# Inverse deviations of all norms: Ln and Exp on ScalarE in place of a power on GpSimd, with a refitted order

## Chip, cores, metric

The kernel runs on one core of a Trainium2 chip. The metric is device time in microseconds (us) of one execution. The core's engines are PE (TensorE), DVE (VectorE), ACT (ScalarE), POOL (GpSimd) and SP (SyncE, which here only issues DMAs). They run side by side, each in its own fixed order, and wait for each other through semaphores.

## What is computed

Four layers with pre-normalisation over x of 8 batches x 1024 rows x 128 columns, all in float32:

```python
def _layernorm(x, axis=-1, eps=1e-05):
    m = jnp.mean(x, axis=axis, keepdims=True)
    v = jnp.var(x, axis=axis, keepdims=True)
    return (x - m) / jnp.sqrt(v + eps)

x = x + L0_attn(_layernorm(x))   # A: linear attention with decay, 16 heads, a scan over the rows
x = x + L0_ffn(_layernorm(x))    # B: mixture of 8 experts, the best 2 of each row, hidden 352
x = x + L1_attn(_layernorm(x))   # C: conv of 3, silu, selective scan with 16 states, gate
x = x + L1_ffn(_layernorm(x))    # D: mixture of 8 experts (best 2) and 2 shared ones, hidden 128
```

So there are 32 norms, four for each batch; the change touches `1 / sqrt(v + eps)` of each.

## The kernel before

**Stages.** The letters A, B, C, D stand for the four layers. A and C take one batch after the other. B and D run as jobs of one or two batches: the rows of a job are sorted by expert into blocks of 256 slots. For a job, the rows are normalised, the gates computed, the rows scattered to DRAM by indirect DMAs of POOL (`m_scatter`, L866), each block's rows and its expert's weights loaded by SP, multiplied on PE (L908 to L910 up, L1062 down), passed through silu on ACT (L1308, L1315), gated on DVE (L1687, L1698), read out by ACT (L1324), stored, and gathered back into x by indirect DMAs of POOL that add (`m_gather`, L885). The D layer of the last batch is computed densely (all experts for all rows, letter E in the norm's names), so that no scatter or gather stands at the end.

**A norm.** `row_stats` on DVE takes means and variances of the 8 row groups of a batch (L1403, L1407) and adds eps (`ve`, 128 x 8, L1409). `inverse_deviation` on POOL (L845) raises this to the power -0.5 (`rstd`). `shifts` on DVE (L1413) makes -mean x rstd. `normalise` on ACT (L1170) writes x x rstd + shift. Four steps of the order belong to it: `s_stats`, `s_rstd`, `s_shift`, `s_norm` (with m_ for the jobs and d_ for the dense batch).

**The order.** `ORDER` is a string of 4944 letters. Each letter names a chain of steps (A a batch's attention, P a job's preparation, C the selective scan's stage, G the gathers and so on), and each occurrence takes the chain's next step. `program` goes through the resulting plan once for every engine, and each engine takes the steps that it has a function for. So the string fixes the order on every engine, POOL's and SP's queues too. A step that waits holds everything behind it on its engine.

**ScalarE's tables.** An activation function needs its table in the engine; the compiler puts a table load ahead of an activation whose table isn't there (`ACT_TABLE_LOAD`). The softplus of stage C (`c_soft`, L1268 and L1270) is an Exp and then a Ln; the decays (L1279) and the gate scores (L1292) are Exp.

**Waits around the change.** `rstd[s].sem` counts one for each inverse deviation of a layer; `shifts` and `normalise` wait for it. On POOL the power waits for `veps`.

Of the kernel before, what the change touches and what calls it, by code (L numbers as in the profile page):

```python
# [41 lines left out]
class BankUses:  # L42
# [37 lines left out]
    "RALsSMUqKoPNVskLAZkVULUPqoSRMTPsVMUAwoTsLwXXkAVkPoUXKPqUXsLSqAosUKwkAeLqkwoAVXVMSSTkoUqAswXeLUoXwqsPPsAoUqNA"  # L80
    "VkoswAPsNLwoqZwRAVUUqLZsVqwPSowTUeAXPsMqqosULewKwqKANVosUPAAoZPLRPRPqUKMAswqwVVTwwUUAwLPeAAPNLZAPUTANeRLSVMP"
    "KSVUAPLAZUPVPGMUeSTSNPKPAZPPVPGULSPRPAPUNLePGeVARTKAAMZAAUNLSAAPUAPZAVAPGRALeRUATAMLVUNVXTAXAUoVUeKUANLSMZVo"
    "sLskoGAUKqSeUsoALkUqwRANsqRKLZGVGoVTMwsUkoMTqAkKRLUUAVwULkGVZoXsXqoAsTewVUAUNkLsLMKqoUAVqCTCUkXoMwsLUAkeswCw"
    "CwLqoAVUoCCqRSAXSqsqCCZVSwoCCsACUosLUCwCsCCXAXLXKCXCCoCqCNCCVCCZCACAwwCsCqwSoqMXbTcqNXUAsXURZAbLdSVdCwqUewVw"
    "xAwhcwKXXxTeAdNXAAAhbAAbAPLAXApZAMxAUAPcSpALAAxAeAUAbVhXAdVAPpNAUcLXZddAoPhxoysZAKbSNhRyxTMABGcekVRboqKSpcUR"
    "scTNpMdbPUehePLVAqyLyUUkRPsKxLwwopkVMPysPhTZbcRoUUALdPxpPVAKNVTUSZqcPbhNUSLModdyVxqLsKUPAPeUpPVycRThLMbLUoxZ"
    "VswUAkeRUhNLZwdVTqKqUMoRUwbNdsVxLTkAepUVoMLZesqwUkAUVGykocGbsVAwLqsoKNRdqKkhwwMUSATpysUxoweSTUVARbpcKqULZoGe"
    "yLNqhVdRwULsAKsUyoZxsxAwVVbMNULSoeLATqMcUUhbqGZLMTwdpRqNGKoswyVVcUqUswUAeqNVpSTcVUZyhKxwdwALLMUUcpNVyALSZwSG"
    "RALSAPeAUhKAARRPpAAAPKVPeZLyKxUTVUMPUAVPLAPAThPUeUTLNpVMyMCRPPGCPULPVPZACSAUCPUCLCPNLVUCCPVUACCTCPCCAKACMPCC"
    "eULZCXCCXCXXAPCPCXLCAVCCCAAXRXCTACXPCACACKNMoCoAZssobSUAVeCNUCVqUbqPVsULoALXUxLRwPZeNdXcqxPPSkRXoXbUZhAPSMsT"  # L90
    "kSKxdNVedVZboRcSkApLuuhUkllvSeKxTMdNsvhpdAqZwpcTbcyUqyxUwSsnXbLoUKdcAMVkLhSXVLXnhUdykxapeobXLVKUcwXXypcVyshA"
    "NkdsbxZoqXUbPwqRAphcdowNSULUZwsAVRxkTRyLUxwKTeMoULbAebqdsVpUUVqBMwPsoLVPchRTZKNxeSVUNLphPUMRVqLqKwAUcyxZodpP"
    "bTMUyhUNcLsVPAyobSSdsPKpPeRLdAVcUwLUqxLwbeoPUMhTZVRysVAUpcKwhLqVUeSNZTUyxuVRKGhwvpLSuTxMNqswlZlSNyddoeZyGUGc"
    "GMvpqbAhGdLScnsaRnbUwVURKpUxeLVyqTLchMUpxwUKVNyUVULNZRehATKUVLLMypAZAVGUCeCCLUCwAVGRUGCLSCATMNKTVACRSZUUACLN"
    "AVPePUGAKCRMCVSTZLUCCNMUCLUZCeSAPVVLRPUVTULUTCKVMKMUCCVPLAPGCCLPUCUCTSUCMPPKPPCeGPPCPULVCLNPGPCUCPCCCCeAPCCK"
    "ZNRVZPUcTbNLRULeVUUMbXLAXKNVUCVAxZhdcdxZdXSAebAAeXRbXAPpLAAhxUALPTAcpMXAAKVAdoUTPbXVAcMUhNosXSVbyRdXULxLShpy"
    "AUVSsxUopdyLZNAPkXVsZceecxuloSSNUPbvhVZbhqKuNkAnxLSZsyluvdqnoppcyxXudlbRblhvwebcPhPyTxdXaMvwAUXPnhdUSpXLXPcq"
    "oxPnsUXPKTVXphLwsyPcKbKdekXPURaMpLkAcVxPoXGBkRUGqLwbysAcVPqUqphRNGTwKRSZeMoxddpUKAVhyLTcxMeNUbZTRkwMoLkUSVLT"
    "AesNpbVsyyKqcwGRKhZdMqRoNMZTRqGAVSkwNspxeUyoeTAGchqbZMexKGTVULyNdwcMdphxywVoGhpLwepSGZNULKsUsTRAMKySLeyoeCAV"
    "CCSKqsTqSCNRZRMUKowAZCeURVCNLwTGqeKCMVGZwLsUMNoLqTsCZAqKwRwCoVCUseTCGKwSCCqMCwSLPCCCDVSPPZeNTVMCCeCGUCKPCCPU"  # L100
    "GCCGPCCLVGCKCPPGCLNPPeVKCPPKNGSPPBZRPTeeCRCCPMNcRcZTNZPUbRPdMxSGbdZSRLNVPSUbMLhKMTSUXdbexTSVGhdUNRLZxXLXTVNp"
    "VdUKcpRcZhXKTMbPyXLMpTSUSZZLMxVNeZXNhpbdyNVPxcUcLxPPSePhXbeuXpXbVchyPpyXbyXbddXSZXxXPhXpxPlZdycbdXNXcxybycxc"
    "hpxPdXvPubcPhySpulSKnuhpRvvhPxpyylncdxTbUdldhvbMRnLUcyRpanRThxdbpxMXVRUTchGMLcyGGULapUVhKdxphUyeNyZeGSTyMpVL"
    "CRVCGCULUCCCULNTKZVUMKKCSGUVeTNSULCCVCCCURCMRLCLeCCZGUCVPVLUCCCKCeNCCZCRVCCCGUGSTZNCeRLCSUVMUGUCNCLUCKTCGPMe"
# [1668 lines left out]
```

## Time and profile before

| | us |
|---|---|
| median of 3 runs | 1686.34 (1683.7 to 1690.24) |
| the profiled execution, its own time | 1692.46 |
| its span | 1690.1 |

The page's second part shows the span in 40 slices of 42 us; each digit is the busy share in tenths, PEclk the clock granted to PE in tenths of full speed:

```profile
PE   6778999998999869989896578789577865857788
DVE  6897887989997879869994887689689488757946
ACT  2313455467657746676546565685645763576551
POOL 1104040872742864638688768610578567763686
PEclk9997999999999989998998689899878988988999
```

A busy share is a mean over a slice: it says which engine a stretch is near to be filled by, not which wait ends last in it. ACT and POOL wait for others much of the time.

### The profile page before, as it was taken

Reading aid. Unit: us, or ns where it says so; the run is one execution under the profiler, and the core shown is the slowest. Engines: PE = TensorE matmul, PEld = TensorE weight load, DVE = VectorE, ACT = ScalarE, POOL = GpSimd, SP = SyncE. Lnnn points to the kernel's source line nnn. Section 1 sums busy time; section 2 is a strip of 40 time slices with the busy share of each in tenths; the row PEclk is TensorE's granted clock in tenths of the full one; section 3 lists DMA queues with packets and bytes.
Section 4 is the critical chain, followed back from the end, with each engine's and each line's share of the span. In section 5 each row is a group of like instructions: output and inputs, shape, how many; then the busy total and the mean of one; then the engine's idle time right before and its main releaser. Section 6 shows DMA issues by size and latency. Waiting matters only on the chain.

```text
span 1690.1 us, 29123 instructions
## 1 busy us (share of the span) xinstructions
PE 1368.6 (81%) x9192; PEld 921.8 (55%) x9192; DVE 1369.1 (81%) x2543; ACT 944.7 (56%) x1667; POOL 924.9 (55%) x544
## 2 busy tenths in 40 slices
PE   6778999998999869989896578789577865857788
...
DVE  6897887989997879869994887689689488757946
ACT  2313455467657746676546565685645763576551
POOL 1104040872742864638688768610578567763686
PEclk9997999999999989998998689899878988988999
...
GB/s 276 259 11 98 112 182 162 208 173 281 281 248 138 266 196 282 247 210 257 234 219 174 243 241 225 303 299 272 168 266 230 165 207 270 224 220 214 301 126 69
...
## 3 DMA queue, kind: packets, MB, share of 16 engines
...
## 4 chain that ended last, share of the span: by engine, by line
issue 14%; PE 10%; DVE 8%; POOL 8%; DMA 6%; ACT 5%; SPq 1%; POOLq 0%; DVEq 0%; ACTq 0%
POOL x L885 6%; DMA x<-outs,slot_idx 3%; DVE arena_c L1521 2%; DMA arena_c<-bc_rows 2%; POOL rows L866 2%; PE bank L1097 1%; PE bank L1117 1%; DVE arena_c L1516 1%; DMA xg<-rows 1%; DVE arena_c L1507 1%; PE bank L1062 1%; PE bank L990 1%; PE bank L1106 1%; PE bank L908 0%; ACT yrow L1324 0%
## 5 line engine op out<-in xcount | busy, mean ns | idle before, releaser
L885 POOL DMA_INDIRECT x<-outs,slot_idx x240 | 487.8, 2033 | 180.8 <-issue 89.3
L866 POOL DMA_INDIRECT rows<-xrow,slot_idx x240 | 350.9, 1462 | 249.6 <-ACT xrow L1226 94.8
L990 PE MATMUL bank<-arena_c,ident 128*128 128x512 f32 x512 | 270.2, 658 | 73.2 <-DVE arena_c L1507 73.2
L1521 DVE TENSOR_TENSOR_SCAN arena_c<-arena_c 128x1024 f32<-128x1024 f32 x128 | 295.3, 2309 | 1.5 <-ACT arena_c L1279 0.7
L908 PE MATMUL bank<-xT_ring,mix 128*128 128x128 f16 (+1 forms) x1296 | 243.9, 226 | 52.9 <-DVE mix L1698 16.5
L909 PE MATMUL bank<-xT_ring,mix 128*128 128x128 f16 (+1 forms) x1296 | 243.2, 225 | 0.0
L910 PE MATMUL bank<-xT_ring,mix 128*128 128x128 f16 (+1 forms) x1296 | 243.1, 225 | 0.0
L1062 PE MATMUL bank<-mix 128*128 128x128 f32 (+1 forms) x1296 | 183.3, 286 | 34.6 <-ACT yrow L1324 22.5
L1062 PEld LDWEIGHTS bank<-mix 128*128 128x128 f32 (+1 forms) x1296 | 166.7, 198 | 69.5 <-issue 64.5
L908 PEld LDWEIGHTS bank<-xT_ring,mix 128*128 128x128 f16 (+1 forms) x1296 | 139.9, 108 | 97.9 <-issue 69.4
L990 PEld LDWEIGHTS bank<-arena_c,ident 128*128 128x128 f32 x512 | 97.7, 208 | 169.3 <-DVE arena_c L1507 87.9
L941 PE MATMUL bank<-arena_a,Wv 128*128 128x512 f32 x256 | 149.1, 666 | 29.5 <-DVE arena_a L1459 28.5
L1303 ACT COPY xT_ring<-bank 128x512 f16<-128x512 f16 x156 | 90.7, 582 | 135.9 <-PE bank L1037 135.5
L1324 ACT ACTIVATE yrow<-bank,xg 128x128 f32<-128x128 f32 x312 | 96.9, 363 | 120.8 <-PE bank L1062 114.8
L1516 DVE TENSOR_TENSOR arena_c<-arena_c 128x1024 f32<-128x1024 f32 x128 | 154.6, 1211 | 7.9 <-DMA arena_c<-bc_rows 4.8
L1507 DVE TENSOR_TENSOR arena_c<-arena_c 128x1024 f32<-128x1024 f32 x128 | 157.4, 1233 | 4.1 <-DMA arena_c<-bc_rows 3.1
L1279 ACT ACTIVATE arena_c<-arena_c,A_w 128x1024 f32<-128x1024 f32 x128 | 143.9, 1145 | 27.0 <-DVE arena_c L1521 24.7
L950 PEld LDWEIGHTS bank<-Wo,arena_a 128*128 128x128 f32 x1024 | 132.5, 199 | 46.0 <-DVE arena_a L1466 23.2
L950 PE MATMUL bank<-Wo,arena_a 128*128 128x128 f32 x1024 | 141.9, 287 | 17.7 <-DVE arena_a L1466 17.0
L909 PEld LDWEIGHTS bank<-xT_ring,mix 128*128 128x128 f16 (+1 forms) x1296 | 139.9, 108 | 21.2 <-issue 19.9
L910 PEld LDWEIGHTS bank<-xT_ring,mix 128*128 128x128 f16 (+1 forms) x1296 | 140.1, 108 | 0.0
L1698 DVE SCALAR_TENSOR_TENSOR mix<-bank,winv,mix 96x256 f32<-96x256 f32 (+1 forms) x156 | 73.8, 474 | 66.4 <-ACT mix L1315 58.0
...
## 6 DMA issues: line engine op xcount, KB each, us to landing
arena_c<-bc_rows SPq DMA_DIRECT2D x256, 512.0 KB, 5.6
...
rows<-mix SPq DMA_DIRECT2D x3, 2580.0 KB, 13.2
```

Of the source, the lines that this page charges most:

```text
L866: pool.indirect_dma_start(out=xs_d[q % ROW_SETS], out_offset=bass.IndirectOffsetOnAxis(ap=slot_idx[:, q % RJ, c, j:j + 1], axis=0), in_=xr ...
L885: pool.indirect_dma_start(out=x[:, b, j, :], out_offset=None, in_=y_d[q], in_offset=bass.IndirectOffsetOnAxis(ap=slot_idx[:, q % RJ, c, i ...
L908: pe.matmul(o, hi, xh, start=True, stop=False)
L909: pe.matmul(o, hi, xl, start=False, stop=False)
L910: return pe.matmul(o, lo, xh, start=False, stop=True)
L941: filled(f"A{b}.v{k}", pe.matmul(fill(f"A{b}.v{k}"), Wv[:, f, :], half(normA, h), start=True, stop=True))
L950: last = pe.matmul(bank[A_BANKS[1]][:, rows], qs[:, k % RQ, rows], Wo[:, f, :], start=(f == 0 and j == 0), stop=(f == EF - 1 and j == TH - 1))
L990: last = pe.matmul(bank[C_BANKS[h]][:], ident[:], half(hb[:, n % RR, :], h), start=(n == 0), stop=(n == NS - 1))
L1062: last = pe.matmul(o[:, j * P:(j + 1) * P], h_ring[n % RH][0:rows, at:at + P], w2(q, k, j)[0:rows, c, :], start=(c == 0), stop=(c == NC[s] ...
L1507: dve.tensor_tensor(hb[:, n % RR, :], hb[:, n % RR, :], Cb[:, g % RB, :], ALU.mult).then_inc(c_prod.sem, 1)
L1516: dve.tensor_tensor(hb[:, n % RR, :], Bb[:, g % RB, :], w, ALU.mult).then_inc(c_dBx.sem, 1)
L1521: dve.tensor_tensor_scan(hb[:, n % RR, :], dA[:, n % RDA, :], hb[:, n % RR, :], 0.0, ALU.mult, ALU.add).then_inc(c_scan.sem, 1)
```

## The change

The power on POOL goes, with its constant -0.5. ScalarE takes its place: Ln of the variance plus eps, a wait for that Ln, and Exp of -0.5 times it, in the same place. Each inverse deviation now adds two to the semaphore, and who waited for one waits for two. Nothing else of the arithmetic changes. All three steps (`s_rstd`, `m_rstd`, `d_rstd`) move from POOL's program to ACT's.

```diff
-        neg_half = sb("neg_half", [P, TT])
...
-        rstd = {s: signal(f"{s}_rstd_done", 1) for s in "ABCDE"}
+        rstd = {s: signal(f"{s}_rstd_done", 2) for s in "ABCDE"}
...
         def _(pool):
...
-            pool.memset(neg_half[:], -0.5).then_inc(s_cons0, 1)
...
-            def inverse_deviation(s, b):
-                wt.wait_ge(veps[s].sem, veps[s].at(nth_of(s, b), 1))
-                pool.tensor_tensor(rstd_b[s, b % 2][:], ve_b[s, b % 2][:], neg_half[:], ALU.pow).then_inc(rstd[s].sem, 1)
...
             def normalise(s, b, dst, done, tiles):
-                wt.wait_ge(rstd[s].sem, rstd[s].at(nth_of(s, b), 1))
+                wt.wait_ge(rstd[s].sem, rstd[s].at(nth_of(s, b), 2))
...
+            def inverse_deviation(s, b):
+                logs = rstd_b[s, b % 2][:]
+                wt.wait_ge(veps[s].sem, veps[s].at(nth_of(s, b), 1))
+                act.activation(logs, ve_b[s, b % 2][:], ACT.Ln).then_inc(rstd[s].sem, 1)
+                wt.wait_ge(rstd[s].sem, rstd[s].at(nth_of(s, b), 1))
+                act.activation(logs, logs, ACT.Exp, scale=-0.5).then_inc(rstd[s].sem, 1)
...
             def shifts(s, b):
-                wt.wait_ge(rstd[s].sem, rstd[s].at(nth_of(s, b), 1))
+                wt.wait_ge(rstd[s].sem, rstd[s].at(nth_of(s, b), 2))
```

The order string is replaced as a whole. It has the same letters, each as many times; 615 of its 4944 places hold the same letter, the rest are mostly shifted by a few places. Its first line was and is:

```diff
-    "AAAAAAAAAAPAAAAWAAAAAAAWAAAAWAAokAksoWAosqkWAoskksqAoqwAskAwoWwAqqwAwsoqAsowqkkswAwoqsoqsowAsAAwAoqwwqossoAq"
+    "AAAAAAAWAAAAAAWAAAAAAAWAWAAAAAAoAsAoAAsoWqqosWswoAqsAowkqwskAqoqwkskoAqswwkkoAAqskwoqsAokwAAwwAAswowqsoAqqso"
```

## Rows read from the trace of the kernel before

**Rows 1.** the page, part 1, and part 4, the chain by engine.

```profile
PE 1368.6 (81%) x9192; PEld 921.8 (55%) x9192; DVE 1369.1 (81%) x2543; ACT 944.7 (56%) x1667; POOL 924.9 (55%) x544
...
issue 14%; PE 10%; DVE 8%; POOL 8%; DMA 6%; ACT 5%; SPq 1%; POOLq 0%; DVEq 0%; ACTq 0%
```

**Rows 2.** stages of 100 us: busy us of each engine (instructions), granted clock, DMA.

```profile
400.00:500.00 100.00, 92.91 (x801) 70.66 (x801) 99.93 (x124) 58.86 (x99) 47.12 (x15) 1.00 0.86 263
...
900.00:1000.00 100.00, 65.70 (x318) 42.22 (x318) 73.34 (x164) 64.46 (x112) 79.43 (x53) 0.74 0.78 226
...
1200.00:1300.00 100.00, 62.45 (x270) 33.51 (x268) 82.65 (x76) 58.74 (x76) 81.86 (x48) 0.78 0.78 236
```

**Rows 3.** what DVE waited for: us, times, longest.

```profile
DVE mix L1698 <- ACT mix L1315: 58.0, 33, 4.2
...
DVE arena_c L1498 <- ACT arena_c L1270: 16.2, 5, 7.0
...
DVE shift_C L1413 <- POOL rstd_C L845: 11.8, 7, 7.5
...
DVE shift_D L1413 <- POOL rstd_D L845: 6.9, 2, 5.2
```

**Rows 4.** chain of waits, its longest piece: start us, us, what.

```profile
1104.20 79.12 issue
```

**Rows 5.** time line, batch 7 norm C: start, us, instruction [idle].

```profile
1467.61 0.17 DVE L1409 TENSOR_SCALAR ve_C<-mv_C 128x8 f32<-128x8 f32 x1
...
1467.87 1.67 POOL L845 TENSOR_TENSOR rstd_C<-ve_C,neg_half 128x8 f32<-128x8 f32 x1 [7.61 <-DVE ve_C L1409]
...
1469.58 0.17 DVE L1413 SCALAR_TENSOR_TENSOR shift_C<-mv_C,rstd_C 128x8 f32<-128x8 f32 x1 [0.37 <-POOL rstd_C L845]
```

**Rows 6.** POOL by line: busy us, mean ns, idle before.

```profile
L845 POOL TENSOR_TENSOR rstd_B<-ve_B,neg_half 128x8 f32<-128x8 f32 x8 | 17.3, 2166 | 20.4 <-DVE ve_B L1409 20.4
...
L845 POOL TENSOR_TENSOR rstd_C<-ve_C,neg_half 128x8 f32<-128x8 f32 x8 | 14.3, 1789 | 120.4 <-DVE ve_C L1409 120.4
```

**Rows 7.** time line at two shifts that waited for POOL's queue.

```profile
885.62 0.29 DVE L1409 TENSOR_SCALAR ve_C<-mv_C 128x8 f32<-128x8 f32 x1
...
897.91 0.17 DVE L1413 SCALAR_TENSOR_TENSOR shift_C<-mv_C,rstd_C 128x8 f32<-128x8 f32 x1 [7.53 <-POOL rstd_C L845]
...
1223.01 0.17 DVE L1413 SCALAR_TENSOR_TENSOR shift_D<-mv_D,rstd_D 128x8 f32<-128x8 f32 x1 [5.15 <-POOL rstd_D L845]
```

**Rows 8.** time line of ScalarE behind the softplus of batch 5.

```profile
1208.28 1.06 ACT L1270 ACTIVATE arena_c<-arena_c 128x1024 f32<-128x1024 f32 x1
1209.35 1.28 ACT L1279 ACT_TABLE_LOAD   x1
1210.65 1.15 ACT L1279 ACTIVATE arena_c<-arena_c,A_w 128x1024 f32<-128x1024 f32 x1
```

**Rows 9.** ScalarE by line, two of the table-load groups.

```profile
L1279 ACT ACT_TABLE_LOAD x64 | 82.1, 1283 | 1.2
...
L1315 ACT ACT_TABLE_LOAD x42 | 53.9, 1283 | 13.4 <-PE bank L910 12.6
```

**Rows 10.** time line of ScalarE at the start.

```profile
9.53 0.20 ACT L1154 ACTIVATE tanh_base<-cols 128x1 f32<-128x1 f32 x1 [7.45 <-DMA Wo<-in_Wo]
9.63 0.19 ACT L1155 ACTIVATE half_b<-cols 128x1 f32<-128x1 f32 x1
9.86 1.26 ACT L1170 ACTIVATE arena_a<-x,shift_A,rstd_A 128x128 f32<-128x128 f32 x3
```

**Rows 11.** time line of POOL, powers ahead of a gather.

```profile
1318.66 1.67 POOL L845 TENSOR_TENSOR rstd_C<-ve_C,neg_half 128x8 f32<-128x8 f32 x1 [8.13 <-DVE ve_C L1409]
...
1324.72 1.60 POOL L885 DMA_INDIRECT x<-outs,slot_idx  x1 [0.17 <-issue]
```

**Rows 12.** DVE by line, the row statistics.

```profile
L1403 DVE BATCH_NORM_STATS2 row_sums<-x 128x6 f32<-128x128 f32 x256 | 52.3, 277 | 5.0 <-DMA x<-in_x 4.9
```

**Rows 13.** what PE waited for.

```profile
PE bank L1037 <- DMA xg<-rows: 26.1, 13, 11.0
```

More of the change, by code:

```diff
@@ L80 @@
[L80 to L104, printed above, removed]
@@ L120 @@
-    "GQIFJZIFOGFOGQJFQOIGOFGIJOGFFQQIFOGJOGFIOIGIFQOOFOIJGIJFJOFIGIQJOIQIQOJQJQJQQJQJQGQQ"
+    "AAAAAAAWAAAAAAWAAAAAAAWAWAAAAAAoAsAoAAsoWqqosWswoAqsAowkqwskAqoqwkskoAqswwkkoAAqskwoqsAokwAAwwAAswowqsoAqqso"
+    "AWqoAswwwsoqqwwsPAqWAAAwPAWAWAPAPAAAAAAAAAAAAAAAWAkosAAAkoPkqPsoPwqAsoqwAsPoAqskoqkPowssoAkqkswoAPPwkqPPAAwq"
+    "woAwssAoqsowqqosswqCwoAwqAswPoqAswAoAwqsqAPwPwWPAAAAwAAAAPPAAAAAPAAWXXAAXPWWAAAAXkAoCAAskosXKXoKPqAqXoXsAAPo"
+    "seXqkwPwqAkwAweAoAsPoRXsosqoksAwkPPqkwwoqPAsPCoAqwqswoPRsqowqRsAwAwToAUsqoTsPqKkwqUAMLMVLUTVAUwsNMwoqUUPwsLA"
@@ new lines @@
+    "TRqLweVRVPUUNMZLKAAATLVUARUMATUwSULeVAVZAPNMUCLPPKARVeNZLTPAUUKALAARVPMAeVPPZAAUARXXVAAULAAAVAKUALKNUAUSXZos"
+    "TLPMUkAqoVRKNXLZkXAsULSPVTXUPqoMUAkwVTMsALoSPSwsXVkXRUoKqsPqeUALoXUwAKwskSqoAXkUTVVLeAoswoPqUwsksMAPUqNoqAVo"
+    "XkLwRsPLANswoqZULZVwUAqswqVoPSwsTqUPqAoesqUwwKLARNoKRMVUPAsPAoPwXZLPqUseAqVLwTKMeVwwAUNwAPPLZUeAASRAAMTLUPVK"
+    "VNPSULAZPeVPSUPPMPGZSUVKTNAGPPLUGPPSLGPRRAUPeVGePNKAASGTAUARMZAAULPNAZPAAAALVUPAAMLeRVKVAoTUNXAUUVTVUeAeoZsL"
+    "NALsUMUoqXsoAkkGKUqsVwGLARKoXXLZNVRSTsoqwMUTAURkUAUVKwMqLoLkksVZAKSqTLkLwoUsVeXsUCNAKkMXVRUqwqCToUAULoAsMXKw"
@@ new lines @@
+    "CkLwsqCqwUACVCLowCSosCqeACVqZoCCUACssosUXwCoSCCXAXCCCNSCCqZCCLXVXCCCCACAsoSRwCwwqbcqXwTSXNMAZVbUUqeLdXsAwXCK"
+    "XwqAxhUcwwxXpAThddVAAbANeALeAcPASAZAAMAUbpAxAAALAhcAXAdVxVbApAPeZUGdNAdoPhAxyUANLoRhyysxTcZqVbMApPUpoRbKTRcL"
+    "eRbMesNPychKUPdAqVPsLpoSVPwxMUwkTbUsyULPkhUZkeALPPoNAdUTxNVcRUKdVhZykMLSpLUdqoVxPAbsUqpPLVRKPSPohbyTMwLUxVZU"
+    "eAkUcwRNhsKLdZbdVqoMqdRTUkcBwGUsNLVeASxkKTpVwUceosqUAULRVZoSysKsbAGwVLoNTMqkwhAwUqypxsUowVGUAqbUZpRSdVeRoseL"
+    "qcLNywhKMGUTsAoKSxUVZyAwLVxbGMoNsceULTZAhMLqUUqLdSwZTpKRMNobcwVsVUqGqywsAUqdTeVNUpLVwUKLcwyhxUAUSLSpNZcMVSRA"
@@ new lines @@
+    "wLAPyRShAPAAUKAepZPRxAyPSLAVUhTKMUPALVAeUKVAPLVTUUpPTeNMPMyPPCCVRPLPUCCPZAACUCVAULPPNLUCPUACVCCTPCCACCPKAMLC"
+    "eCZUCGXCCCPXCPXCCAACCAVCCLATAPCRXCCAXCoXCANMKAoXZbbNCsAUsoUVCVPRUqULAVsLNLXUeoxZPwcqdXSRPkXPkZxAdehSUosbKPNV"
+    "BTxqMSekVXXoXZAubRucpLhvXSUdlTlXxMdNsdSwUvXhXApKkcXqpyyeqTxUXbwLUZcAsonebdcVUKhVkMLLShbdxcnapVLPwyoUpVbKcsyh"
+    "kUNxbosyRALUqddqSUpZwSAeGRowZwRVsxNAxTkLeKhyGUwToVqMUkALbsbdpVqPUcwsMLoUVTRhVKPwZLNUexpNPhMULVqxdSqhUZcAcGoK"
+    "eyTPULpRysbVUMPNbKASoswLRdcPpdPyAUVUebLwLqwGxoMTPUhcSyRcVsVAUTpZNKGhqULVUxLVyGheZMuRSvSpwuTNxqwKslNoZGvyyblG"
@@ new lines @@
+    "UddpeGcqZAShGRScMsdTnnaUbwVURpxULMecVqhLpyKLUxwUAKRVNyUKVULZehTVNLeLpAwMZAUCVyRUCCULCSACVUTAMKLNCATCUUACACCV"
+    "ZRLPPSMNULeZeVTUACKCRSRUNVKCMLVUGZCPUTSLUVUTVPVKCLMMUCLCPULAPCPCCUPTGUCVKVMCPAPCPPPPULeCNPLCCPeUCCCPACCPKNRZ"
+    "TUVCbNPUCeZLSMUXLRUbXKAXVAVCcLxeVNhcXZRdxdXdAPbAUSZAALXAAbLpUXhAePPxAAcpTKMAcAVXdyPUbTUMAobyVhUosSVdLcLNxXkR"
+    "hASdUpyVUsxeoXNXbLZpuVseAPNxoSZlUbqvhScZuVNhxpsLyovAZSnuKlddlyXRwucpnbkqxclhevbyxPSPhTdaMAPbUXUnXvchdSpLqKox"
+    "XKnUPPLTcBVpskKyXbPXhsadUeMPXRpLPVkwoAxRRkPUwccRyqbLAPsZUqpVqNhToxwMKdeKbdepUAVyTLhMNxoUkcZRpTMbwVLyUTXAwekN"
@@ new lines @@
+    "VGASqcswsKLoMhRdZyVTZKeSqMqZNRSRxsUNypMoTLqcAGhbwweTxUKywNcKyepdGVMhSTxeVohedpLpsKwRZNsUALUoLVyyKSZkeCACTMCG"
+    "SKRNKsCeUVqoRwNZqMCMZLRqTAUCLGVCwsUNSZGoqseVMGKTCKqLGRwosAKCwVTSweqMUGCCCwCwGCKBSCCDSPGPLGUNGVTZCCNGCUeCMCCC"
+    "PPCLCCPPPGeCCVCPLGCPKCPNPePGCSVPKPRGNTZCRPcNZCPePxZMGTMcdGSUZVPRbPbNhdSLRUKZTXTbMLMXxUURSNVhexddLeRLTpKSbTXV"
+    "pVSZdcUMUPhRNcyMTpKbSLxSMVNZehNXZNXLPSypVbxcXUdcexZPPPLehbpbdXVcbXhpXbxuPXKXPydXyXcZddyxySXySlNyPbZhXcdcpXSb"
+    "bXxXhPPPxcpulcxyvRPbhulpnuhpyvhvnxdydbplxTcUhddcnyRMRRvpLahRUnUxphMTcLVXbTULxyKdcaRyUpUVhxpNhGpZyTyGVGCCMGUe"
@@ new lines @@
+    "GVeLPCSLCUUCMLNCTUKVZMKKUCTNVCeURRVLCSCGCUCCCMGGLVULCZCCSCUCCNVLeCCKCZTUeGRSCeCZGRVNCLCSMCCUVUUCCNUTCLCKVebM"
+    "bCPGUGUVVZPLLccKLSxVUbUNxdGRTLhMKVUebPKVUUTyZLxpNLchpRUPdBxbVdPZhTMdULyLUPcVMRNxUGUbeUKZpGLbPVdyhPcxpecLNTUb"
+    "MeRPKVxSULyhZcbVpVdcdhpUTdKNhLyPTUGVMUSbUxShcMRpyLZpcdVNbyxeVLUZeRSPLhUcbUTGdKxyPVbcuLpVeNMhpdKxddyhlZPyTNux"
+    "bvPphbnUyvxZMplcRUdcPUVhxLnKxUydpPePdTLcVShRLUbVUVLcMyKaUNLpPhUUyuyLlSSVpTVZxMhSvupleUZyRNCvReCLCUCNSKeSKUCC"
+    "ZTnnVULCCeVaMUNTPCKGKCCLCUCMCPZVCCCUPCLCXCCPXCCVUXCCNCSCVXCCCCCLLCXSCbxVZUXcbcbhebdcPxpdhexhpKdyxpbNdcbxXcPb"
@@ new lines @@
+    "XXyXhdpXhxPcXZbPdhXdccPdPpPXyySpPSxbhXuXKpXvKyxebehydlbPucXlcpbPevxuhdyyxchuvnRRclpxdRPdyRPpxyTURdTblnvMMTLh"
+    "MhbULTpaKXVpndcecUynxyVBKNhbaLTpUMKdxdhVeZMybNpRcLPPKcZUVRVGxLMShpSZyZTxNNRMSULVGhZNTULRMZeeVTKpyNRUMTVLNZKS"
+    "yRGSeCCUKRLCNCMTCSVCZKULTMRSNTZCVCPUKMSNCCRCUTCKCPCePLMZRTPLCVMCPCPUGNPeZGSTPGeMKeVGCCPCVNGGUCPGKRKGPGVGLPGP"
+    "ZSCSGLCCeCPCUePNCCNCSLRRPVCSZTTCUMZPKMCCNbPuNBSRZPTKLXVcCblvcXxudhUdlpRbMLcvxhUbeLXTeybVpXXndxdGunXMbbhZKpud"
+    "clNZSNxecVTveKbUayvXhMXbXxylcxShKyhdxNdpVcnLSUcpexXbZyneKhSXpayxhSyephcbdVeZxcXSppdNLZKXbXxcyyXhbRTpRdhcxXpd"
@@ new lines @@
+    "XRTdUbxTUXhpcMdMVLbhRcRyLpNKxdZyVMUhdeRXTNKbpcyeMTZUSVNLxyVLhpcMRGUZeGNSxhdLKZyTeVURKRMySZpLRKNyCCGTMVCGNeKC"
+    "TSRUKMCZMTLUCGTKNLGMCPUCTPSCCUVKKVRCVPNZSCCLReLMGZeCCCGCNRZeCCTVCCMSCCGCeCGTeSNGCCUZLCRVCMGCCULVCSTGMTKUCbCU"
+    "bVZGLNNMPULKPRPLVVxxZcRePuSldZbPNvPhpGNxPdduSPKGSNbdZhPcZhxTMcbTRhPUSRPcTlPyRKppMPvPbKnLMxPdcdUpSeXyeKnPGyca"
+    "beVBUeXhVTXLXZbKyNxcXpuxTMVuLSlddUbMKhevehGSveXlNcLxNpXUZynVpbLnVXNSXyxaZbhpSyXSdydcZdcNybxKxTXZhSbcRecpRdhd"
+    "MpdxbeRMKhhGpcRcGReUxLbpTMyyxThMdbUcGVphTyTKKpyLUcNUNGNeLMUZRVZLSyZVTxydUKxMLRhTNySVKpRehGVpKRCVCCCMNUZCNELS"
@@ L121 @@
+    "KZTeMGZERGeSVMLUSEMTTNULUSeEZGVENRKEVGSLEGuZNeVTveuLlENRZUlMGEvVSSnnTuZNLuGUEalZvvnVMnlFFJESLaIOJIFNEOFOFIOZ"
+    "GFOFGOSFGOFFFOSOFIOGFOOGFOFOFGOGGGGGJGGIQJQQIJOJQIQJQJJJIQJQQIJQIJQGQIJGQJQJQQQIIIII"
 )
@@ L820, in ready @@
                 pool.iota(blk_i, pattern=[[1, NBT * MOST_BLOCKS]], base=0, channel_multiplier=0).then_inc(s_cons0, 1)
-                wt.wait_ge(s_cons0, 9 + len(run))
+                wt.wait_ge(s_cons0, 8 + len(run))
                 for m in run.values():
@@ L889, in m_gather @@
                         compute_op=ALU.add).then_inc(gathered[i] if c else gathered_first[j], 16)
-            program({"top": top, "d_rstd": d_rstd, "c_bias": c_bias, "ready": ready, "s_rstd": inverse_deviation, "m_rstd": m_rstd, "m_scatter": m_scatter, "m_gather": m_gather})
+            program({"top": top, "c_bias": c_bias, "ready": ready, "m_scatter": m_scatter, "m_gather": m_gather})
         @block.tensor
@@ L1171, in normalise, with d_rstd, m_rstd @@
                                    scale=rstd_b[s, b % 2][:, j:j + 1]).then_inc(done, 1)
+            def inverse_deviation(s, b):
[4 more added lines that the diff above has]
+                act.activation(logs, logs, ACT.Exp, scale=-0.5).then_inc(rstd[s].sem, 1)
+            def d_rstd(b):
+                inverse_deviation("E", b)
+            def m_rstd(q, i):
+                inverse_deviation(JOBS[q][0], JOBS[q][1][i])
             def s_norm(s, b):
```

29 lines of the change are left out of this document (3 added, 26 removed).

## The prediction

> **What bounds the kernel now.** The executed profile is 1692.5 us, its span 1690.1; the median of three runs is 1686.3, so what I add to the profile I add to the median as well. I read the engines' busy times first [rows 1]: PE and DVE stand at 81% each, ACT at 56%, POOL at 55%. No engine is full over the whole, so the stages come next [rows 2]: from 400 us DVE is busy 99.9 of 100 us and the sum there is DVE's; from 900 and 1200 us neither PE nor DVE is over 83%, and PE's granted clock is 0.74 and 0.78, means between its two levels of 1.2 and 2.4 GHz. There the time is made of waits between engines, and a longer wait costs. Then the waits of DVE and PE [rows 3, 13]. On ACT, DVE waits 58.0 us for the last silu of a block and 16.2 us for the logarithm of the softplus; with the smaller rows of both engines' lists I add up 122 us for DVE and 62 us for PE, 184 us in all. For the norms, DVE waits at the shift 11.8 us (C), 6.9 us (D), and 3.4, 1.9 and 1.8 us (B, E, A): 25.8 us.
>
> The chain of waits passes over POOL for 8% of the span and has 14% "issue" [rows 1]. I don't take this as POOL's price: its longest "issue", 79 us [rows 4], ends at the norm of C at 1183 us, where POOL stood in its queue for a variance that DVE had not reached. That is a wait of POOL, not for POOL.
>
> **What a norm costs now.** In the plain case [rows 5] the variance is ready at 1467.78, GpSimd's power runs 1467.87 to 1469.54, DVE's shift starts at 1469.58: 1.8 us from one DVE step to the next. All 32 powers make 65.6 us of POOL (two of the five groups are in [rows 6]). In two of them POOL was late because its queue came first [rows 7]: the C norm at 897.91 (variance ready at 885.91, five more gathers issued ahead of the power) held DVE for 7.53 us and ACT for 7.66; the D norm at 1223.01 held them for 5.15 and 5.17. Take these 12.7 us from 25.8, and the other norms cost DVE 13.1 us.
>
> **The change: ScalarE's tables.** The new pair is Ln and then Exp. In this program a logarithm and an exponential stand in different tables: after Ln at 1208.28 the very next Exp pays a table load of 1.28 us [rows 8], and each of the eight Ln has a load of its own right behind an Exp. The count comes from the order string: I wrote the steps out in its sequence, kept ScalarE's Exp, Ln and Silu (Tanh and copies need no load beyond the first), and counted each change. For the old string this gives 166, what the trace has (64 at the decays, 42 and 22 at the silus of a block, 13 at the shared ones, 8, 8, 6 and three single ones [rows 9]). The new string gives 237: 71 more, 91 us. Most norms fall between two silus, so that a silu load comes back behind them: 80 at the block silus where 64 were. The 64 small activations take about 0.2 us each (0.19 and 0.20 for one column [rows 10]), 13 us. ScalarE gets 104 us of new work, from 945 to 1049 us, 62%.
>
> The Trainium skill ("ScalarE: Activation LUTs", section on table sets) says that one set holds both exp and ln and that the pair needs one load. The loads in the softplus speak against it [rows 8]; rival (c) below is what its rule would do here. The same page gives a drain of about 1.38 us beside every switch, which would add about 98 us more of ScalarE by its figure; in [rows 8] Ln ends at 1209.34 and the load starts at 1209.35, and the next activation starts 0.01 us behind the load, so no such drain shows here.
>
> **The norm's own path.** Two loads, two small activations and three hand-overs of under 0.1 us: 1.28 + 0.2 + 1.28 + 0.2 + 0.2 = 3.2 us against 1.8. The load waits with its activation (in the trace a silu's load has the same releaser as the silu), so it isn't hidden in the wait. At the very start it is worse [rows 10]: ScalarE is held by the attention weights until 9.53 and done with its two constants at 9.82, where POOL had worked meanwhile. The first norm's shift moves from 9.04 to about 12.9 and the first normalisation from 9.86 to 13.2: 3.3 us, with nothing beside it.
>
> For the others I summed DVE's work that the string puts between variance and shift, with the durations of the trace. Against 1.8 us the old string leaves 15.5 us uncovered (13 norms); the trace has 13.1, so the method reads a little high. Against 3.2 us the new string leaves 28.0 us for 12 norms and 5.7 for the first, 33.7 us, scaled 28.5. DVE's idle time at the shifts thus goes from 25.8 to 28.5 us, **+3 us**: the two queue waits on POOL (12.7) pay for most of the longer path.
>
> **What queues behind it on ScalarE.** Each pair takes 3 us of ScalarE and often a silu load after it; behind it stand the turns of the next block's rows, the silus and the output rows, for which DVE and PE wait. Bounds: 0, if all 104 us fall into ScalarE's 745 us of idle time; at the top 52 us, if waits grow as load over idle share does (0.56/0.44 to 0.62/0.38, 28% of 184). I take growth in step with the work, 104/945 = 11% of 184: **+20 us**, as a third of the pairs lie in the first 300 us, where ScalarE is lightly loaded.
>
> Of these 23 us of idle time I let 0.8 reach the end, the busy share of PE and DVE: +18 us.
>
> **What POOL gives back.** Its queue loses 65.6 us and the waits for variances, at which ready gathers stood: ten such norms, 66.6 us, as at 1318 us (8.13 us; the next gather starts 0.17 behind a second power) [rows 11]. But who waits for gathers? DVE's row statistics have one idle time in the whole trace, 4.9 us for the input [rows 12]: never for a gather. The string leaves the C statistics where they were (steps 953, 1593, 2141, 2726, 3143 of 4944; now 945, 1589, 2148, 2727, 3147), so the earlier gathers aren't used. Scatters do matter: PE waits 26.1 us for rows of blocks [rows 13], and eight powers stand among scatters, 2 us each. With the last gathers at the end that is 18 us at most and 0 at least; I take **-8 us**.
>
> Removed memset and one semaphore count: nothing. The string itself is refitted only locally (the softplus of batch 7 is step 4424, was 4422); I give it no gain of its own.
>
> **Sum:** 18 - 8 = +10 us, profile 1702, median **1696 us**.
>
> **The rivals.** (a) POOL's queue is what sets the pace of the waiting stages. For it: gathers held 66.6 us, POOL 79 to 82% busy from 900 and 1200 us. Against: [rows 12]. Price: the 12.7 us of the two queue waits and about 10 us for 65.6 us of power at POOL's share of the chain (8 of 55%), less the start's 3.3 and some of ScalarE's cost: 1672 us. Chance 0.20. (b) ScalarE's idle time covers all but the start: 1686 + 3, less a little at the tail: 1688. Chance 0.22. (c) One load serves Ln and Exp, against [rows 8]. The same count over the string, with one table for the pair, gives 195 loads; the norm's path is 1.9 us, about POOL's, and ScalarE gets (195 - 166) x 1.28 + 13 = 50 us, 5% of 184 us or 10 us of waits, which POOL's 8 us about cancel: 1686. Chance 0.04. This is what the Trainium skill's page on ScalarE gives for such a pair. (d) The longer silu paths bite in the stages of [rows 2] where waits rule, PE idles more and its clock, 0.74 where PE is 66% busy and 1.00 where it is 93%, sinks further: the top bound, (52 + 3) x 0.8 = 44 us, less 8 for POOL: 1722 us. It decides from the point where a silu load stands ahead of every second wait of DVE at the block gates. Chance 0.10. The forecast has 0.44; its own range is 1690 to 1704.
>
> **How the numbers follow.** About 0.5%, 8.4 us, is what can be told from no change here. Slower by more: (d) and 0.33 of the forecast, 0.43. Faster by more: 0.18 of (a) and 0.02 of (b), 0.20. Within: the rest, 0.37. Range: from (a), 1670, to 1714, between the forecast's upper end and (d), whose upper half I leave out with the fastest cases.
>
> **What would show it.** 237 table loads in the changed trace (195 would be (c)); Ln about 0.2 us; ScalarE near 1049 us; POOL near 859; first normalisation at 13.2 us; DVE's idle time at the shifts near 28 us and at the silus above 58; no idle time of 7.5 us ahead of a C shift. Wrong: idle times of DVE at the silus unchanged with ScalarE up by 100 us (then (b)), or the C and D stages starting tens of us earlier (then (a)).

## The result and the profile after

| | before | changed |
|---|---|---|
| median of 3 runs | 1686.3 us | 1731.5 us (1727.8 to 1734.1) |
| ratio | | 1.024 (95% interval 1.021 to 1.028) |
| span of the profile | 1690.1 us | 1732.4 us |

The change makes the kernel 2.4% slower, and the span is longer by 42.3 us. The first part of the page of the changed kernel (busy us by engine) answers to [rows 1]:

```profile
PE 1393.4 (80%) x9192; PEld 936.5 (54%) x9192; DVE 1359.9 (79%) x2543; ACT 1045.1 (60%) x1802; POOL 866.9 (50%) x511
```

ScalarE has 100 us more, POOL 58 less. DVE works 9 us less, so its idle time has grown from 321 to 372.5 us: by 51.5 us, of which 42.3 are the loss. PE needs 25 us more for the same matmuls, at a mean granted clock of 0.906 instead of 0.916. The loss is spread over the whole run: the changed kernel is 4.2 us behind at the shift of the first norm, 12.2 us at the variance of the first C norm (352.41 us), 24.7 us at 705 us, 31.6 us at 917 us and 40.3 us at the last norm (1653.99 us).

The groups of ScalarE's lines that hold table loads (answering to [rows 9]: count, busy us, mean ns, idle before them):

```profile
L1280 ACT ACT_TABLE_LOAD x59 | 75.7, 1283 | 1.1
...
L1316 ACT ACT_TABLE_LOAD x51 | 65.4, 1283 | 5.4 <-PE bank L898 4.5
...
L1166 ACT ACT_TABLE_LOAD x32 | 41.1, 1283 | 0.6
L1164 ACT ACT_TABLE_LOAD x30 | 38.5, 1283 | 20.2 <-DVE ve_A L1410 19.7
L1309 ACT ACT_TABLE_LOAD x29 | 37.2, 1283 | 7.6 <-PE bank L898 7.0
```

L1164 is the Ln, L1166 the Exp of a norm, L1316 and L1309 are the silus of a block, L1280 the decays. With 13, 8, 7, 6 and two single ones these are 237 loads, 71 more than before. The waits of DVE (us, times, longest), answering to [rows 3]:

```profile
DVE mix L1699 <- ACT mix L1316: 78.6, 37, 8.5
...
DVE mix L1688 <- ACT mix L1309: 15.3, 9, 3.7
DVE shift_C L1414 <- ACT rstd_C L1166: 14.1, 6, 3.1
...
DVE arena_a L1433 <- ACT arena_a L1242: 11.1, 4, 8.4
...
DVE shift_A L1414 <- ACT rstd_A L1166: 7.1, 2, 6.0
```

The silu of a block's last chunk keeps DVE waiting 78.6 us (58.0 before), that of the first chunks 15.3 (5.4). At the shifts it is 14.1 and 7.1, with 5.3 for D and 4.5 for B: 31.0 us instead of 25.8. And PE waits for ScalarE too (the 14.2 us below are one wait at the very start):

```profile
PE bank L896 <- ACT mix L1309: 17.2, 14, 4.5
PE bank L913 <- ACT arena_a L1158: 16.9, 5, 14.2
...
PE bank L1025 <- ACT xT_ring L1304: 16.3, 11, 3.8
```

**Where it goes, at one norm.** Time lines of ScalarE and of DVE in the changed kernel, norm D of batch 1 (start us, us, instruction, idle before it):

```profile
737.95 1.28 ACT L1309 ACT_TABLE_LOAD   x1
739.24 0.69 ACT L1309 ACTIVATE mix<-bank,winv 128x512 f32<-128x512 f32 x1
739.95 1.28 ACT L1164 ACT_TABLE_LOAD   x1
741.24 0.21 ACT L1164 ACTIVATE rstd_D<-ve_D 128x8 f32<-128x8 f32 x1
741.47 1.28 ACT L1166 ACT_TABLE_LOAD   x1
742.76 0.21 ACT L1166 ACTIVATE rstd_D<-rstd_D 128x8 f32<-128x8 f32 x1
742.88 0.57 ACT L1304 COPY xT_ring<-bank 128x512 f16<-128x512 f16 x1
743.47 1.28 ACT L1316 ACT_TABLE_LOAD   x1
744.76 0.47 ACT L1316 ACTIVATE mix<-bank,winv 96x256 f32<-96x256 f32 x1
```

```profile
739.97 0.75 DVE L1688 SCALAR_TENSOR_TENSOR mix<-bank,winv,mix 128x512 f32<-128x512 f32 x1 [3.15 <-ACT mix L1309]
745.34 0.48 DVE L1699 SCALAR_TENSOR_TENSOR mix<-bank,winv,mix 96x256 f32<-96x256 f32 x1 [4.62 <-ACT mix L1316]
747.95 0.75 DVE L1688 SCALAR_TENSOR_TENSOR mix<-bank,winv,mix 128x512 f32<-128x512 f32 x1 [2.13 <-ACT mix L1309]
748.62 0.15 DVE L1414 SCALAR_TENSOR_TENSOR shift_D<-mv_D,rstd_D 128x8 f32<-128x8 f32 x1
```

ScalarE never stands still here: between two silus of blocks lie the pair (3.0 us) and a load to come back to Silu (1.28 us). DVE idles 3.15, 4.62 and 2.13 us for silus. It doesn't idle for the norm itself: the shift at 748.62 found its inverse deviation done at 742.97. At the same norm in the kernel before, DVE idled 1.77 us for a silu ahead of the shift at 714.21 and 0.41 behind it. The shift itself is a poor clock here, since the new order puts three gates of blocks ahead of it (two L1688 and one L1699) where the old one has one (L1698). The gates, counted off in both traces, tell more: the last one ahead of the pair of norms is 24.7 us behind its counterpart (728.13 against 703.47 us), the four from 739.97 us on are 31.0 to 31.6 us behind. So the C and the D norm together lost 6 to 7 us here.

### The profile page after: what moved, and what is told of

Its sections match the earlier page's. It is cut to its first block, busy times and chain, and to the rows that moved or that the text cites. A ratio compares the mean times of both kernels' runs of the same rounds, so it can differ in the third digit from the quotient of the medians.

```text
span 1732.4 us, 29230 instructions
## 1 busy us (share of the span) xinstructions
PE 1393.4 (80%) x9192; PEld 936.5 (54%) x9192; DVE 1359.9 (79%) x2543; ACT 1045.1 (60%) x1802; POOL 866.9 (50%) x511
## 4 chain that ended last, share of the span: by engine, by line
PE 31%; DVE 22%; ACT 16%; issue 13%; DMA 9%; POOL 5%; SPq 3%; DVEq 0%; POOLq 0%; ACTq 0%
PE bank L978 4%; DMA arena_c<-bc_rows 4%; POOL rows L854 4%; DVE arena_c L1522 3%; DVE arena_a L1449 3%; PE bank L1050 3%; DVE arena_c L1517 3%; PE bank L929 3%; DVE arena_c L1508 3%; PE bank L896 2%; PE bank L938 2%; PE bank L898 2%; PE bank L897 2%; DMA xg<-rows 2%; DVE arena_a L1460 2%
## 5 line engine op out<-in xcount | busy, mean ns | idle before, releaser
L854 POOL DMA_INDIRECT rows<-xrow,slot_idx x240 | 375.9, 1566 | 562.6 <-DVE slot_idx L1673 256.0
L873 POOL DMA_INDIRECT x<-outs,slot_idx x240 | 466.7, 1945 | 244.0 <-DMA outs<-yrow 151.1
L896 PE MATMUL bank<-xT_ring,mix 128*128 128x128 f16 (+1 forms) x1296 | 250.8, 229 | 65.3 <-ACT mix L1309 17.2
L1522 DVE TENSOR_TENSOR_SCAN arena_c<-arena_c 128x1024 f32<-128x1024 f32 x128 | 291.6, 2280 | 4.6 <-ACT arena_c L1280 3.8
L898 PE MATMUL bank<-xT_ring,mix 128*128 128x128 f16 (+1 forms) x1296 | 250.0, 229 | 0.0
L897 PE MATMUL bank<-xT_ring,mix 128*128 128x128 f16 (+1 forms) x1296 | 250.0, 229 | 0.0
L1050 PE MATMUL bank<-mix 128*128 128x128 f32 (+1 forms) x1296 | 187.9, 291 | 35.8 <-ACT yrow L1325 21.8
L896 PEld LDWEIGHTS bank<-xT_ring,mix 128*128 128x128 f16 (+1 forms) x1296 | 142.7, 110 | 117.8 <-issue 66.0
L1517 DVE TENSOR_TENSOR arena_c<-arena_c 128x1024 f32<-128x1024 f32 x128 | 161.9, 1269 | 25.7 <-PE bank L978 13.4
L1508 DVE TENSOR_TENSOR arena_c<-arena_c 128x1024 f32<-128x1024 f32 x128 | 155.2, 1215 | 12.3 <-DMA arena_c<-bc_rows 11.4
L897 PEld LDWEIGHTS bank<-xT_ring,mix 128*128 128x128 f16 (+1 forms) x1296 | 142.8, 110 | 22.7 <-issue 21.1
L1280 ACT ACTIVATE arena_c<-arena_c,A_w 128x1024 f32<-128x1024 f32 x128 | 143.9, 1145 | 16.7 <-DVE arena_c L1522 16.0
L938 PEld LDWEIGHTS bank<-Wo,arena_a 128*128 128x128 f32 x1024 | 131.5, 198 | 31.4 <-issue 19.7
L898 PEld LDWEIGHTS bank<-xT_ring,mix 128*128 128x128 f16 (+1 forms) x1296 | 143.0, 110 | 0.0
L1699 DVE SCALAR_TENSOR_TENSOR mix<-bank,winv,mix 96x256 f32<-96x256 f32 (+1 forms) x156 | 73.5, 473 | 85.7 <-ACT mix L1316 78.6
```

The source lines that it names most:

```text
L854: pool.indirect_dma_start(out=xs_d[q % ROW_SETS], out_offset=bass.IndirectOffsetOnAxis(ap=slot_idx[:, q % RJ, c, j:j + 1], axis=0), in_=xr ...
L873: pool.indirect_dma_start(out=x[:, b, j, :], out_offset=None, in_=y_d[q], in_offset=bass.IndirectOffsetOnAxis(ap=slot_idx[:, q % RJ, c, i ...
L896: pe.matmul(o, hi, xh, start=True, stop=False)
L897: pe.matmul(o, hi, xl, start=False, stop=False)
L898: return pe.matmul(o, lo, xh, start=False, stop=True)
L938: last = pe.matmul(bank[A_BANKS[1]][:, rows], qs[:, k % RQ, rows], Wo[:, f, :], start=(f == 0 and j == 0), stop=(f == EF - 1 and j == TH - 1))
```

## The experiments

Ratios are against the kernel before, with 95% intervals. The theory at the outset (T): ScalarE's new work, table loads above all, costs the time. Against it: the refitted order (O), ScalarE standing at a variance with work behind it (H), the norm's longer path.

### The pair in the old order

The changed kernel, with the string `ORDER` of the kernel before put in the place of its own; nothing else is altered:

```diff
-ORDER = (
-...
+ORDER = (
+...
```

> The changed kernel's Ln and Exp on ScalarE with the order string of the kernel before; complete arithmetic. Theory T (tables and ScalarE's occupancy cost the time, whatever the order): about 70 table loads more than the 166 of before, as in the changed kernel, and 1.02 to 1.04 times before; DVE's wait for the silu of the last chunk (58.0 us before, 78.6 changed) also about 75 or more. Rival O (the refitted order is what is slow, the pair itself is cheap): within 1% of before.

Measured: 1.050 (1.044 to 1.057), with 241 loads, more than T had expected. The pair costs more in the old order; the refit had won back half. DVE waits 80.7 us for L1316. O falls.

### No power at all, old order

```diff
-dve.tensor_scalar(ve_b[s, b % 2][:], mv_b[s, b % 2][:, :, 1], EPS, None, ALU.add).then_inc(veps[s].sem, 1)
+dve.tensor_scalar(rstd_b[s, b % 2][:], mv_b[s, b % 2][:, :, 1], 0.0, 0.25, ALU.mult, ALU.add).then_inc(rstd[s].sem, 1)
```

The call of `inverse_deviation` and its steps on POOL are taken out too. Every inverse deviation is thus 0.25, and neither POOL nor ScalarE works for a norm.

> Order of before. Left out: the power (DVE writes 0.25 + 0 x variance into the inverse deviation in the place of variance + eps, so no engine computes it and the norms are only scaled by a constant). This tells what GpSimd's power and its place in POOL's queue cost before. If they set the pace (rival a of the prediction): 0.98 or less, 1655 us. If they are hidden, as DVE's idle time of 25.8 us at the shifts suggests: 0.985 to 1.0.

Measured: 0.994 (0.991 to 0.997). GpSimd's power with its place in the queue, and the 25.8 us that DVE waited for it at the shifts, cost 0.6% together, some 10 us, and no more was to be had. Rival (a) of the prediction, that POOL's queue set the pace, falls.

### Two copies in the place of Ln and Exp, old order

```diff
-act.activation(logs, ve_b[s, b % 2][:], ACT.Ln).then_inc(rstd[s].sem, 1)
+act.activation(logs, ve_b[s, b % 2][:], ACT.Copy).then_inc(rstd[s].sem, 1)
...
-act.activation(logs, logs, ACT.Exp, scale=-0.5).then_inc(rstd[s].sem, 1)
+act.activation(logs, logs, ACT.Copy).then_inc(rstd[s].sem, 1)
```

DVE writes a constant into `ve` in the place of the variance, so each norm is scaled by that constant.

> Order of before, inverse deviation on ScalarE, but both activations are copies, which need no table (166 table loads as before; left out: the power, the norms are scaled by a constant). It keeps the waits for the variance, the two steps and the hand-over, without 2.6 us of loads. Theory T: close to before, 0.99 to 1.005, since only loads cost. Rival H (ScalarE standing still for a variance, with all its other work behind it, is the cost): 1.015 or more.

Measured: 1.002 (0.998 to 1.006). Everything but the loads is here: the wait for the variance, two activations, hand-overs. Against the kernel before it is free within the interval; against no power at all it costs 0.8 points, as much as GpSimd's power did or a little more. H falls, and of the 1.050 of pair_old_order some 4.8 points (81 us) hang on 75 table loads, 96 us.

### A pair that nobody waits for

```diff
+            def idle_pair(*args):
...
+                act.activation(spare[:, 0, :], A1[:], ACT.Ln).then_inc(s_base, 1)
+                wt.wait_ge(s_base, 2 * n + 3)
+                act.activation(spare[:, 1, :], spare[:, 0, :], ACT.Exp, scale=-0.5).then_inc(s_base, 1)
```

> The kernel before, complete, with GpSimd's power in use; in addition ScalarE runs a pair of Ln and Exp on a tile of ones at each place of an inverse deviation. It waits for no variance and nobody waits for it: occupancy and loads alone. Theory T: most of the loss of pair_old_order, 1.015 to 1.03. Rival H, or the longer path of the norm as the cause: below 1.01.

Measured: 1.044 (1.037 to 1.050). Nearly the whole loss of the pair, though the norms come from POOL as before and nobody waits for this result. It is above T's range of 1.015 to 1.03. The norm's longer path is not the cause.

### The new order, step by step

The same edits in the refitted order: no power, two copies, and a copy with Exp.

> The refitted order with no power at all (DVE writes 0.25 + 0 x variance as the inverse deviation; nothing on ScalarE). 162 table loads. With the old order the same gave 0.994 of before. Theory T (the loads cost, the order was bent towards them): 0.99 to 1.01, the new order is no worse in itself. Rival O2 (the refit gave up something that counts without the pair): 1.01 or more.

> The changed kernel with its order, Ln and Exp replaced by two copies, no tables (power left out, the norms are scaled by a constant); 162 loads. Theory T: 0.995 to 1.01, so that nearly all of the 1.024 goes with the 75 loads. Rival H2 (in the new order ScalarE stands at variances, 19.7 and 13.9 us in the changed trace, and this costs): 1.015 or more.

> The changed kernel with its order, Ln replaced by a copy and Exp kept (power left out, the norms are scaled by a constant). By my count 198 table loads, 36 above 162, 39 below 237. If each load costs about the same: half-way between copies_new_order and the changed kernel, 1.01 to 1.018. If the cost sets in only past some load of ScalarE: near copies_new_order.

Measured: 0.997 (0.993 to 1.000), 0.999 (0.996 to 1.003) and 1.006 (1.003 to 1.010). So the new order is no worse in itself. From 162 to 198 loads the time rises by 0.7 points (12 us for 36 loads), from 198 to 237 by 1.8 points (30 us for 39). The price of a load isn't constant.

The new order with the power on POOL has no time: with the norms in POOL's queue in that order, the engines would wait for each other in a circle. So what the new string does for GpSimd's power stays unknown.

### Fewer loads in the kernel before

17 decay steps of the old string moved by up to 16 places.

> The kernel before, complete, GpSimd's power in use, with 17 decay steps moved by up to 16 places in the order so that Exps stand together: 133 table loads, 33 fewer than before. Theory T with a price per load that holds downwards too (about 0.97 us each from pair_old_order): 0.98. If removed loads give back less, because a decay moved early or late makes ScalarE or the scan wait: 0.99 to 1.01.

Measured: 1.008 (1.005 to 1.011), with 133 loads, and ScalarE at 900.6 us instead of 944.7. 33 loads fewer and slower, where a constant price per load had asked for 0.98: what the moves cost is not told apart from what the loads gave.

**No silu.** The last way to take loads out leaves the order alone:

```diff
-ACT.Silu
+ACT.Tanh
```

in every place, of the kernel before and of the changed one (a tanh is then computed where a silu belongs):

> The kernel before with Tanh in place of every Silu (this is left out: silu), same shapes and durations. Tanh stands in the table of Exp, so only the softplus's Ln forces loads: 17 by my count, 149 fewer, 191 us less of ScalarE. If a load costs 0.8 to 1 us of time downwards too: 0.91 or less. If the order has hidden most of the loads that it was made for: 0.97 to 1.0.

> The changed kernel with Tanh in place of every Silu (silu is left out). 77 loads by my count, 160 fewer than in the changed kernel. If what counts is ScalarE's sum of work and where the loads stand, the pair's 2.56 us in one piece stays but no silu pays a load behind it: between 0.97 and 1.0 of the kernel before, and within 2% of tanh_for_silu_before. If the pair in one piece is itself the cost: 1.02 or more above tanh_for_silu_before.

Measured: 0.990 (0.985 to 0.995) and 1.011 (1.007 to 1.016). The first parts of the two pages, before's variant first:

```profile
PE 1360.7 (81%) x9192; PEld 921.4 (55%) x9192; DVE 1366.8 (82%) x2543; ACT 746.0 (45%) x1518; POOL 937.3 (56%) x544
```

```profile
PE 1389.5 (81%) x9192; PEld 932.9 (54%) x9192; DVE 1362.7 (79%) x2543; ACT 831.5 (48%) x1642; POOL 879.0 (51%) x511
```

Two things follow. 149 loads fewer, 199 us of ScalarE, gave 17 us: the old order had hidden nearly all of them. And with ScalarE at 831.5 us, 113 us **less** than in the kernel before, the changed kernel's variant is still slower than before, and 2.2% above its own counterpart. ScalarE's sum of work therefore doesn't set the price (my theory T, in its simple form, falls too), and the loads that bring Silu back aren't needed for a loss: without them the changes cost 2.2%, with them 2.4%.

### The same work without a table load

11 more copies of 96 columns behind each pair of copies, each waiting for the last (block_of_copies, the first hunk), and then the same 352 copies spread out (spread_of_copies, the first hunk with 3 in the place of 11, and the second):

```diff
                 act.activation(logs, logs, ACT.Copy).then_inc(rstd[s].sem, 1)
+                fill_time(11)
...
+            some = lambda b, n: fill_time(2 * (n % 8 in (1, 4)))
+            one = lambda *a: fill_time(2)
+            program({"s_stats": one, "m_stats": one, "d_stats": one, "s_shift": one, "m_shift": one, "d_shift": one, "c_prod": some, "a_qs": some,
```

> copies_old_order (1.0019) with 11 small copies more behind each of the 32 pairs, each waiting for the last, about 3 us in one piece (its trace tells how much), 90 to 100 us of ScalarE in all; table loads as before (166). Power left out, the norms are scaled by a constant. Theory P (a piece of 3 us on ScalarE at these places, whatever is in it, is the cost): 1.035 to 1.05, near pair_old_order. Rival D (a table load costs more than the 1.28 us that it shows): 1.01 to 1.02.

> The same 352 small copies, spread over the order: two at the place of each statistics and of each shift, three behind each pair, two at a quarter of the steps of the scans. Same work for ScalarE as block_of_copies. If ScalarE's sum of work is the price: the same as block_of_copies. If the length of the piece is, because the waiting engines have a slack of one or two us: clearly less, under 1.015.

Measured: 1.057 (1.049 to 1.064) and 1.018 (1.012 to 1.025), the second near the 1.015 expected of a slack. The copies in the two kernels' lines of ScalarE, in this order:

```profile
L1167 ACT ACTIVATE filler<-Wo 128x96 f16<-128x96 f32 x352 | 99.0, 281 | 10.1
```

```profile
L1167 ACT ACTIVATE filler<-Wo 128x96 f16<-128x96 f32 x352 | 98.6, 280 | 6.8
```

and the first waits of DVE in each:

```profile
DVE mix L1709 <- ACT mix L1326: 88.8, 40, 9.6
...
DVE mix L1698 <- ACT mix L1319: 33.6, 11, 6.2
```

```profile
DVE mix L1712 <- ACT mix L1326: 74.3, 43, 5.8
...
DVE mix L1701 <- ACT mix L1319: 14.5, 11, 2.7
```

Against copies_old_order the block costs 5.5 points, 93 us for 94 us that ScalarE's busy time rises by: its full length, and more than the 1.035 to 1.05 expected. A rival by which a load costs more than its 1.28 us isn't needed. (A variant with three copies of 1024 columns in the place of the 11 small ones has no time, as its tile doesn't fit into SBUF.) (The Trainium skill, "ScalarE: Activation LUTs", section on what a table load costs, gives each switch a drain of about 1.38 us more. No such drain shows in these traces: the next activation starts 0.01 us behind the load, and copies without any load cost as much as the pair with its loads.) The same copies in crumbs of two or three, 0.5 to 0.8 us each, cost 1.6 points, 27 us: three tenths. But most of the crumbs also stand in other places than the block, so this run alone can't say whether size or place did it.

PE's clock has a part in all this. PE needs 1412.2 us in the block's profile and 1377.9 in that of copies_old_order for the same matmuls, at granted clocks of 0.896 and 0.913. Only ScalarE's work differs, so the slower PE follows from it in some way, but how much of the 93 us would go if the clock stayed is shown by no run.

### Size or place

```diff
-                fill_time(11)
+                fill_time(5)
```

That is half_block_at_norms. block_in_scans has no copies there, and 11 at every fourth product of C's scans:

```diff
+            program({"c_prod": lambda b, n: fill_time(11 * (n % 4 == 2)),
```

> copies_old_order with the same 32 blocks of 11 small copies (3 us each) as block_of_copies (1.057), but placed at every fourth product step of the selective scans and none at the norms. If any burst of 3 us on ScalarE costs its length: 1.05 or so. If the places of the norms are special, because no slack is left there: 1.02 or less, as spread_of_copies (1.018).

> copies_old_order (1.002) with 5 small copies (1.3 us) in place of 11 behind each pair of copies. If the waiting engines have a slack that a burst must exceed first: under 1.015. If delay passes on in proportion: 1.002 + 5/11 of 0.055 = 1.027.

Measured: 1.038 (1.030 to 1.045) and 1.021 (1.013 to 1.029). 3 us in one burst in the middle of the scans cost two thirds of their length (60 us); half a burst at the norms costs about in proportion (32 us for 40 us, with an interval of some 14 us either way). So place counts: bursts cost more at the norms than in the scans, but they cost in the scans too. That length counts by itself isn't shown in the old order. A burst of 1.3 us at the norms is already passed on, at 0.8 us for each us of work against 1.0 for the full block, which the intervals don't tell apart. In the new order a price that grows with the burst is likelier: a copy with Exp makes ScalarE 46 us busier than two copies and costs 12 us, Ln and Exp make it 97 us busier and cost 42.

### In two parts

Exp held back behind up to two table-free steps of ScalarE, in the old order, and the kernel before with its normalisations of A and C and its softplus broken in the same way.

> pair_old_order (1.050), complete arithmetic, with Exp of each pair held back behind up to two following steps of ScalarE that need no table (turned rows, output rows and the like), where such steps follow. Same loads (about 241), same work; one piece of 3.0 us becomes two of 1.5. If the length of the piece is the price: 1.02 to 1.04. If the work is: 1.045 or more. Against it: the shift waits longer for the norm.

> The kernel before, complete, its own longest pieces on ScalarE broken: the 16 normalisations of A and C (3.19 us in one piece) in two halves and the 8 softplus pairs (4.7 us with two loads) in Exp and Ln, with up to two table-free steps between the parts. If long pieces cost in the old kernel as well as in the experiments: 0.985 to 0.995. If its order was made around them: 0.997 to 1.005.

Measured: 1.049 (1.042 to 1.056) and 1.006 (1.004 to 1.008). The first tells little: in its time line only 10 of the 32 pairs have anything between Ln and Exp, 7.3 us in all, so the burst is hardly broken. For the changed kernel with Exp held back there is no time: in that order the engines would wait for each other in a circle. The second is slower, as if pieces for which the order was made are better left alone, but why isn't shown. Neither beats the kernel before, and nor does any kernel of this study that computes the whole result.

## Why the prediction was wrong

The direction and the mechanism were right, that ScalarE's table loads keep DVE and PE waiting; the size was not: +10 us forecast, +45 measured (42 by the profiles), and the range ended at 1714.

- **Tables: right.** 237 loads forecast and found; Ln 0.21 us; ScalarE 1045 us against 1049, POOL 867 against 859. The load stays 1.28 us with the next activation 0.01 us behind it.
- **The norm's own path: right.** 31.0 us of DVE at the shifts, 28.5 forecast. The first normalisation starts at 13.51 us (13.2 forecast), and the shift ahead of it is 4.2 us late. The C norm of batch 3, late by POOL's queue in [rows 7], gives time back: 31.6 us behind at its variance, 24.5 at its shift. The load isn't always behind the wait, as I had it: at three norms ScalarE idles with the load done (15.3 us at two A norms, 2.1 us at a C norm), and at one 19.7 us ahead of the load.
- **POOL's part: not confirmed.** -8 us forecast for the queue alone. No power at all gives -10 us in the old order and -6 in the new, but that takes away DVE's 25.8 us at the shifts as well; at 0.8 of these and 8 for the queue my sum would have asked for -29. With POOL free and two cheap copies on ScalarE the time is that of before (1.002 and 0.999).
- **What queues behind the pair: the step that failed.** I scaled the 184 us that DVE and PE had waited for ScalarE by ScalarE's growth, 11%, and took 20 us. By the full lists, without the shifts, these waits were 127 us for DVE and 68 for PE and are now 161 and 116: 277 us, 82 more, and my upper bound was 52. Of the 82, DVE has 34 and PE 48. Not all of PE's part is new idle time: 14.2 us are one wait at the start, where POOL ended one of 10.5 us before, and PE waits 38 us less for DVE (182.7 to 144.8), so that its waits grew by only 20 us in all. In time, the loads behind the pair cost 42 us in the changed kernel (1.024 less 0.999). The experiments say why the scaling is wrong: ScalarE's sum of work doesn't set the price (199 us less gave 17 us, the spread copies cost three tenths), while 3 us in one burst at a norm cost 2.5 to 2.9 us each in the old order (81 us and 93 us over 32). My reading is that the order leaves the silus and gates little slack there, which a mean share of idle time doesn't show; slack itself was not measured. The same pairs cost 1.3 us each in the new order: the refit, to which I had given nothing, hides half.
- **Where the pairs cost.** I had counted on the first 300 us, where ScalarE is lightly loaded. But the changed kernel is already 12.2 us behind at 352 us, 4.2 of them from the first norm.
- **0.8 of idle time reaches the end: not shown.** 42.3 of 51.5 us of DVE's new idle time is 0.82, but this share is no test: the 51.5 us are the 42.3 us of the longer span and 9.2 us that DVE works less. I had applied 0.8 to the waits of both engines. With the measured 82 and 5 us it gives 70 us, less 8 is 62, not 45: the factor was too high, and hid a part of the error in the waits.
- **Rivals.** (d), the slow end, gave 1722 us, nearest to the 1731.5 measured, and had too low a chance; but its own signs are not met. A table load stands directly ahead of the silu in 16 of the 46 waits of DVE at the block gates (7 of 37 before), not in every second. And the granted clock of the waiting stages hasn't sunk: it is 0.89 from 725 to 1435 us, where it was 0.88 in the like stretch from 700 to 1400; it is lower up to 363 us (0.92 against 0.95) and behind 1435 us (0.86 against 0.89). PE needs 25 us more, but 15 of them also in copies_new_order (1383.2 us), which is as fast as the kernel before. (a), (b) and (c) are out: no power at all gives 0.6% at most, ScalarE's idle time does not cover the pair, and Ln and Exp take two loads.

What stays open: why a burst costs more at the norms than in the scans, how much of the loss goes through PE's clock, and whether a pair that is really broken in two would be cheaper; the run meant for it broke too few.
